# Third batch's residual, statistics and deviation tile by tile, with one weight split moved behind them

## What is computed

```python
x = layernorm(x + attention(x))          # 16 heads of 16, causal, q/k/v/o projections 256x256
x = layernorm(x + experts(x, token_ids)) # expert e = min(clip(token, 0, 12499) // 3125, 3)
                                         # y = (silu(x C_e^T) * (x C_e^T)) C_e^T, C_e = ctx_2048[e], 256x256
x = layernorm(x + moe(x))                # top 1 of 4 by softmax(x Wr + br); F = 1024, weight = its probability
```

## Time and profile before

| | us |
|---|---|
| runs shown, median of 3 | 292.88 |
| runs shown, lowest and highest | 290.88, 294.34 |
| the profiled execution's own time | 293.57 |
| its span on the core | 291.8 |

### The profile page before, as it was taken

One profiled execution on the slowest core, in us unless ns is written; L12 is line 12 of the kernel. 1 busy time (PEld: TensorE's weight loads), 2 busy tenths in 40 slices (PEclk: granted clock), 3 DMA queues, 4 the chain that ended last, 5 costly groups with the idle time before them and its releaser, 6 DMA issues.

```text
span 291.8 us, 7077 instructions
## 1 busy us (share of the span) xinstructions
PE 234.3 (80%) x2714; PEld 189.1 (65%) x2730; DVE 191.7 (66%) x425; ACT 135.3 (46%) x229; POOL 66.1 (23%) x128
## 2 busy tenths in 40 slices
PE   4568678988899897599997346898778999999970
PEld 4356355665676664367796222598768999999960
DVE  4887648786699685569988452789535555556550
ACT  4536355766694885256555151488131333333300
POOL 8500000100020444212122556000113212222222
PEclk9999779999999999789999558999999999999996
DMA  6999244142024444602409412340000000000000
GB/s 189 340 315 318 74 144 152 67 147 72 3 85 135 109 115 177 163 2 72 147 20 403 161 59 81 94 111 2 0 20 20 4 13 20 21 20 20 7 5 15
DMA packets 17424, 28.63 MB, mean 98 GB/s; under 512 B 2733, under 2 KB 12974, under 8 KB 17392
## 3 DMA queue, kind: packets, MB, share of 16 engines
q1 hardware_dynamic: 16048, 25.28, 27.5%
q0 software_dynamic: 1344, 2.90, 2.8%
HBM read 19.43 MB, written 9.50 MB: 99 GB/s over the span
## 4 chain that ended last, share of the span: by engine, by line
PE 56%; DVE 21%; issue 9%; ACT 5%; POOL 4%; DMA 3%; SPq 1%; POOLq 0%; DVEq 0%; ACTq 0%
PE ps L1285 9%; PE ps L1678 7%; PE ps L1679 7%; PE ps L1680 7%; PE ps L1695 3%; PE ps L1697 3%; PE ps L1696 3%; DVE wf_lo L795 3%; PE ps L1362 3%; POOL sorted L519 2%; DVE arena L961 2%; PE ps L1614 2%; DMA ring<-wqkvT 2%; PE ps L1358 2%; ACT wf_hi L559 1%
## 5 line engine op out<-in xcount | busy, mean ns | idle before, releaser
L1678 PE MATMUL ps<-arena,wf_hi 128*128 128x128 f16 x352 | 60.2, 219 | 0.3 <-DVE arena L1197 0.3
L1679 PE MATMUL ps<-arena,wf_hi 128*128 128x128 f16 x352 | 60.3, 218 | 0.0
L1680 PE MATMUL ps<-arena,wf_lo 128*128 128x128 f16 x352 | 60.2, 217 | 0.0
L1679 PEld LDWEIGHTS ps<-arena,wf_hi 128*128 x352 | 34.3, 98 | 0.2
L1678 PEld LDWEIGHTS ps<-arena,wf_hi 128*128 x352 | 33.7, 96 | 0.9 <-issue 0.8
L1680 PEld LDWEIGHTS ps<-arena,wf_lo 128*128 x352 | 33.9, 96 | 0.0
L1695 PE MATMUL ps<-wf_hi,arena 128*128 x88 | 24.0, 273 | 5.9 <-DVE arena L1222 3.4
L795 DVE SCALAR_TENSOR_TENSOR wf_lo<-ring,wf_hi 128x1024 f16<-128x1024 f32 x17 | 20.6, 1219 | 11.0 <-ACT wf_hi L559 5.9
L751 ACT ACTIVATE arena<-ps 128x512 f32<-128x512 f32 x22 | 13.1, 594 | 29.7 <-PE ps L1680 29.7
L1697 PE MATMUL ps<-wf_hi,arena 128*128 x88 | 24.0, 273 | 0.0
L1696 PE MATMUL ps<-wf_lo,arena 128*128 x88 | 24.0, 273 | 0.0
(11 more groups left out here) (223 smaller groups left out, 562.8 us busy)
## 6 DMA issues: line engine op xcount, KB each, us to landing
ring<-Wf SPq DMA_DIRECT2D x17, 512.0 KB, 3.7
sorted<-fill SPq DMA_DIRECT2D x1, 4515.0 KB, 20.8
arena<-Wf SPq DMA_DIRECT2D x7, 512.0 KB, 8.1
arena<-sorted SPq DMA_DIRECT2D x20, 129.0 KB, 2.3
sorted<-fill SPq DMA_DIRECT2D x1, 1161.0 KB, 6.3
ring<-xT SPq DMA_DIRECT2D x4, 256.0 KB, 5.1
X<-x_tok SPq DMA_DIRECT2D x1, 1024.0 KB, 7.8
ring<-ctxT SPq DMA_DIRECT2D x2, 512.0 KB, 3.6
```

What stands on the lines that cost most here:

```text
L1678: t.matmul(dst, hi, a_hi[p][:, k], start=k == 0, stop=False)
L1679: t.matmul(dst, hi, a_lo[p][:, k], start=False, stop=False)
L1680: last = t.matmul(dst, lo, a_hi[p][:, k], start=False, stop=k == NK - 1)
```

## The change

VectorE, third batch: in step 14 the residual, the statistics and the aggregation are done for tile 0 and then for tile 1 (`third_out`), and right behind them the two deviations (`third_norm`), which were in step 15. Of the two splits of step 13 the first stays and the second is done in step 15, so behind the deviations. POOL makes rstd of the third batch tile by tile, as for the last one, and sends the batch's two scatters behind the second power. The semaphore values that the last batch waits for rise by one. Nothing that is computed changes.

```diff
--- before.py
+++ after.py
@@ -494,15 +494,18 @@
             g.memset(QT[0][DK * 2:SLOT, 1::2, :].bitcast(F32), 0.0).then_inc(row_z, 1)
             pool.wait_ge(filled, 32)
             pool.wait_ge(pos_rdy, 1)
-            for b in range(B - 1):
+            for b in range(B - 2):
                 pool.wait_ge(mv1, TB * (b + 1))
                 inv_std(mv[:, :, 1], TB, rs1)
                 if b == 1:
                     for j, at_ in enumerate(DENSE_AT):
                         g.tensor_copy(XS[:, at_, D:D + 2], X1[:, NA + j, D:D + 2]).then_inc(id_rdy, 1)
                 scatter2(b)
-            for j in range(TB):
-                tt = NA + j
+            for j in range(2 * TB):
+                tt = NA - TB + j
+                j %= TB
+                if tt == NA:
+                    scatter2(B - 2)
                 pool.wait_ge(mv1, tt + 1)
                 link(g.tensor_scalar(veps[:, j:j + 1], mv[:, j, 1:2], EPS, None, ALU.add))
                 g.tensor_tensor(rstd[:, j:j + 1], veps[:, j:j + 1], minus_half[:, 0:1], ALU.pow).then_inc(rs1, 1)
@@ -994,6 +997,24 @@
                     v.scalar_tensor_tensor(out=X1[:, tt, 0:D], in0=ps[:, project_bank(b), j * D:(j + 1) * D],
                                            scalar=1 / W_SCALE, in1=X1[:, tt, 0:D], op0=ALU.mult, op1=ALU.add).then_inc(res1, 1)
 
+            def third_out(j):
+                tt = TB * (B - 2) + j
+                dve.wait_ge(wo_rdy, TB * (B - 1))
+                v.scalar_tensor_tensor(out=X1[:, tt, 0:D], in0=ps[:, project_bank(B - 2), j * D:(j + 1) * D],
+                                       scalar=1 / W_SCALE, in1=X1[:, tt, 0:D], op0=ALU.mult, op1=ALU.add).then_inc(res1, 1)
+                dve.wait_ge(res1, tt + 1)
+                v.bn_stats(st[:, j, :], X1[:, tt, 0:D]).then_inc(bn1, 1)
+                dve.wait_ge(bn1, tt + 1)
+                if j == 0:
+                    dve.wait_ge(rs1, B - 2)
+                v.bn_aggr(mv[:, j, :], st[:, j, :]).then_inc(mv1, 1)
+
+            def third_norm(j):
+                tt = TB * (B - 2) + j
+                dve.wait_ge(rs1, B - 1 + j)
+                v.tensor_scalar(X1[:, tt, 0:D], X1[:, tt, 0:D], mv[:, j, 0:1], rstd[:, j:j + 1],
+                                ALU.subtract, ALU.mult).then_inc(x1_rdy, 1)
+
             def stats1(b):
                 for j in range(TB):
                     tt = TB * b + j
@@ -1055,21 +1076,28 @@
                 if g == 2 and b + 1 < B - 1:
                     max_T(b + 1)
                 if b >= 1:
-                    if g == project_at(b):
+                    if g == project_at(b) and b < B - 1:
                         residual(b - 1)
                         stats1(b - 1)
                     elif g == 1 and b == B - 2:
                         norm1(b - 2)
-                    elif b == B - 1 and g == 3:
-                        norm1(b - 1)
+                    elif b == B - 1 and g == 2:
+                        for j in range(TB):
+                            third_out(j)
+                        for j in range(TB):
+                            third_norm(j)
                 if stacked_at(step) is not None:
                     stacks(stacked_at(step))
-                for _ in range(min(1, ATT_LO[step])):
+                if b < B - 1 or g != 1:
+                    for _ in range(min(1, ATT_LO[step])):
+                        split_lo(n)
+                        n += 1
+                if b == B - 2 and g == 2:
+                    o_lo(b - 1)
+                if b == B - 1 and g == 1:
                     split_lo(n)
                     n += 1
-                if b == B - 2 and g == 2:
-                    o_lo(b - 1)
-                for _ in range(ATT_LO[step] - 1):
+                elif b == B - 1 and g == 3:
                     split_lo(n)
                     n += 1
                 if projected_at(step) is not None:
@@ -1099,7 +1127,7 @@
                 v.bn_aggr(mv[:, j, :], st[:, j, :]).then_inc(mv1, 1)
 
             def last_norm(j):
-                dve.wait_ge(rs1, B + j)
+                dve.wait_ge(rs1, B + TB - 1 + j)
                 v.tensor_scalar(XS[:, DENSE_AT[j], 0:D], X1[:, NA + j, 0:D], mv[:, j, 0:1], rstd[:, j:j + 1],
                                 ALU.subtract, ALU.mult).then_inc(x1_rdy, 1)
```

## The result

The change made the kernel slower: 295.37 us median (292.72 to 299.09, 20 runs) against 292.88 (290.88 to 295.21, 20 runs), a ratio of 1.0077 with a 95% interval of 1.0049 to 1.0105. Forecast were 293.4 us and 290.6 to 295.0, so the time lies 0.37 us above the range, and the forecast's +0.5 us became +2.5.

The account below looks back on a forecast made before the run. No engine bounds the kernel everywhere; at the hand-over the chain waits for the scatters. Their landing at 117.0 against 116.49 gave +0.5 us: 294.1 from the profiled 293.57, 293.4 us with the median 0.69 below, range 290.6 to 295.0.

Parts of the forecast that it names:

- The residual's start: VectorE, third batch: with one split moved away, the residual starts at about 107.75, 0.61 us earlier than before.
- the split's end within VectorE's idle time: VectorE before the last batch's outputs: the moved split ends at 112.4, before 113.24, and costs nothing.
- the load beside the second scatter: SyncE: the 512 KB weight load waiting for the moved split leaves at about 112.5, 0.05 us behind the second scatter.
- the landing: Third batch's second scatter: lands 4.3 to 5.0 us after its start, not 2.7; taken as 117.0 against 116.49.
- the first transpose: TensorE at the hand-over to the first expert layer: the first tile's transpose comes 0.2 to 0.9 us later.
- Rival 1: Hand-over: the collision costs little, the scatter lands at 115.2, 1.2 us won, 291.7 us; chance 0.28.
- rival 2: First expert layer: Rival 1 holds and TensorE's clock is kept, gain 3.9 us, 289.0 us; chance 0.07.
- rival 4: Hand-over: the landing stays within 0.3 us of 116.49, gain and collision cancel, 292.9 us; chance 0.11.
- The sum: Hand-over: all scatters landed at 117.0 against 116.49, so +0.5 us on the kernel; chance 0.48.
- the way to the second scatter: VectorE and POOL, third batch: second scatter starts at 112.47 against 113.75, 1.28 us earlier.
- the rest of the program follows the transpose: Everything behind the first tile's transpose: it keeps the same distances, so only the +0.5 us carries through.
- Rival 3: First expert layer: TensorE's gap becomes 2.2 us, the slow-clock stretch grows by 2.5 us, 295.9 us; chance 0.06.

Follow-up runs that it names:

- E4: The changed kernel unaltered, measured again on the chip of E1 to E3: ratio 1.0105 to the kernel before, median 2.8 us higher.
- E1: The changed kernel with the weight load beside the second scatter held until behind the tiles' loads: ratio 0.9880 to the kernel before, median 0.8 us lower.
- E3: The changed kernel with both splits left where they were, so only the tile order changed: ratio 0.9992 to the kernel before, median 0.4 us higher.
- E8: The kernel before with only the same weight load as in E1 held behind the tiles' loads: ratio 0.9987, median 0.1 us lower.
- E14: The changed kernel with 11 idle products filling TensorE's gap, repeat of E6 on another chip: ratio 0.9977 to the kernel before, median 0.2 us lower.
- E10: The kernel before with the tiles' loads held for the last batch's first-tile statistics, repeat of E5 on another chip: ratio 1.0047, median 0.4 us higher.
- E2: The kernel before with only the second split moved behind the third batch's deviations: ratio 1.0152, median 4.6 us higher.
- E6: The changed kernel with 11 idle products filling TensorE's gap before the first tile's transpose: ratio 1.0001 to the kernel before, median 0.1 us lower.
- E13: The kernel before with 7 idle products filling TensorE's gap before the first tile's transpose: ratio 0.9859, median 3.5 us lower.
- E11: The kernel before with the tiles' loads held until the last batch's second mean and variance are made: ratio 1.0117, median 3.3 us higher.
- E5: The kernel before with the tiles' loads held for the statistics of the last batch's first tile: ratio 1.0009, median 1.0 us higher.
- E9: The changed kernel unaltered, measured again on the chip of E10 to E12: ratio 1.0133 to the kernel before, median 3.1 us higher.
- E12: The kernel before with only the second split moved, repeat of E2 on another chip: ratio 1.0033, median 3.2 us higher.
- E16: The changed kernel with the weight load held, repeat of E1 on another chip: ratio 0.9846 to the kernel before, median 2.5 us lower.

## Why the prediction was wrong

**Right.** The mechanism and its place. The residual's start was forecast at 107.75 and was 107.76; the split's end within VectorE's idle time, 0.8 us of cover forecast, 0.62 measured; the load beside the second scatter, forecast 0.05 us off, measured 0.07 behind it (E4: 0.13 ahead); the landing 4.3 to 5.0 us after the start, measured 4.78, 4.77 and 4.82 in three profiles; the first transpose 0.2 to 0.9 us late, measured 0.83. E1 shows that it is the load, E3 that it isn't the tile order, E8 that it isn't the load's absence elsewhere. Rival 1 (2.7 to 3.3 us), rival 2, which needed rival 1, and rival 4 are refuted.

**A term that was too small.** The sum was +0.5 and the transpose was 0.83 late. 0.25 of the difference is the landing: 4.78 us and not 4.53 (112.47 to 117.0). The scatter did land 0.4 us after the load beside it, as the prediction had it, but the load itself took 4.3 us and not 4.0. About 0.1 is the way to the second scatter, which began 4.82 us behind the residual instead of 4.72. In this profile POOL's sum for tile 1 took 0.39 us and not 0.23, beside VectorE's first deviation (111.25), which the last batch's rows didn't have. The Trainium skill, SBUF — State Buffer, section Who interferes with whom, lists the `tensor_scalar` among the VectorE instructions that can take the ports that GpSimd shares. Eight of the ten profiles with this tile order fit that with 0.39; in E4 and E14 the sum took 0.23, though the deviation started 0.06 us ahead of it as in the others. And in E4 the second scatter began 4.80 us behind the residual all the same, so the sum alone isn't the 0.1.

**The step that failed** is the sentence of the sum that "the rest of the program follows the transpose" at the same distances. TensorE's clock does not follow. The longer gap was followed by 10.2 us at 1.2 GHz and not 6.8 in the first expert layer. From the first transpose to the last layer's the profiles with 10.2 us took 67.2 to 67.7 us and those of before, E3, E8 and E10 with 6.8 took 66.1 to 66.5: about 1.0 us, in which all but E2's have the beginning of a second stretch at the start of the last layer too. With that one and a third one 22 us on, the changed kernel's last layer took 108.8 to 108.9 us against 106.9, 1.9 us. 0.83 + 1.0 + 1.9 is 3.7 us over the profile before. The medians are 2.5 to 3.1 apart; the kernel before's executions spread too (mean clocks of 0.922 to 0.945 in those of the experiments), but which stretches they have wasn't profiled.

Rival 3 had seen a growing slow stretch. Its condition, a landing after 117.0, was met at 117.35, and the forecast itself had named the gap of 2.2 us, while the earlier trace rows already showed a clock that fell behind a gap of 1.7; a chance of 0.06 was too small. That its time, 295.9, is close to the 295.37 measured is partly luck: it priced the first layer's growth at 2.5 us, which came to about 1.0, and the 1.9 us of the last layer were in no rival. The range ended at 295.0 because rival 3 was left out of it.

**What stays open.** That the gap brings the slow stretch in the first layer is shown by filling it (E6, E13, E14) and, without any collision, by lengthening it (E11); the profiles with gaps of 1.40 to 2.29 us have 6.8 us of it, those with 2.50 and more 10.2, and of two with 0.54 and 0.66 us one has none and one 6.8. Why the last layer's stretches come with a late first tile is not shown, and they are the larger part of the loss. The later one sets in about where TensorE has waited 2.44 us for the last chunk's split, and that wait is as long in the profiles without the stretch (before, E3, E8). It came in all ten profiles of kernels with a late transpose, filled gap or not, and in two of the eight others. That TensorE's idle gap in the first layer isn't its cause is what E6 and E14 say. Of the 3.3 us between E14 and E13, the lateness (0.7) and the last layer (1.9) account for 2.6 at most, if E13's other executions are mostly free of slow stretches there. The difference in mean clock could cover the rest: in these profiles 3.4 us at 1.2 GHz cost 0.9 to 1.7 us, so the 5.7 us are worth 1.5 to 2.8, an estimate, and with the lateness 2.2 to 3.5. And E5 and E10 lost less than the changed kernel with nearly its lateness.

## What to carry to other kernels

A split, a wait or a copy that a load is queued behind moves the load too: look up what the load will run beside at its new time, and leave transfers that nobody needs yet away from the one on which a hand-over waits. A stage change where TensorE stood for 2 us cost more here than the 2 us; count what the clock does behind it, and try idle products in the gap before rearranging the engines that feed it (here 7 of them were worth 1.2% by the medians and 1.4 by the ratio, in six runs on one chip, the whole rearrangement with its load held and the gap filled not measurably more). Where a stretch of the trace is at half clock now, the chance that a small shift makes it longer belongs among the likely cases, not at the edge.

## What the runs showed of the hardware that was not expected

- An indirect DMA of 129 KB from POOL landed in 2.6 to 3.1 us alone, and in 4.0 to 5.0 beside one 512 KB load, whether the load was issued up to 0.5 us behind it (before, after, E9), 0.13 ahead (E4) or 1.2 us ahead (E2, E12); the load itself took 4.0 to 4.5 us, and mostly 3.3 to 3.7 elsewhere.
- POOL's instruction for the first scatter of the third batch took 1.63 us where it started 0.55 us into a VectorE split (E2 and E12), and 1.09 to 1.15 where none ran or the split started after it. A split doesn't always do that: the scatter of 106.98 in the kernel before started 0.88 us into one (106.10) and took 1.18.
- A slow stretch of 3.4 us cost 1.4 to 1.7 us in the last layer (E10, E1, E2, E13), where TensorE is busy throughout (9.97 of 10 us), and 3.4 us more of it in the first expert layer, where it often waits, about 0.9 (E2 against before).
- Gaps of 0.54 and 0.66 us before the same first layer were followed by no slow stretch and by 6.8 us of it: one kernel (E16, E1), two chips, 2.2 us apart from the first transpose to the last layer's.
